# Causal zeros set on GpSimd after the exponential in eleven of sixteen attention steps, instead of by mask matmuls

## What is computed

```
x = layernorm(x + attention(x))        # 16 heads of 16, causal
x = layernorm(x + experts_by_token(x)) # one of 4 by token id
x = layernorm(x + moe_ffn(x))          # router, best of 4 experts, 1024 wide
```

```
scores = einsum('bhqd,bhkd->bhqk', Q, K) / sqrt(16)
scores = where(causal, -inf, scores)        # causal: key index > query index
attn = softmax(scores, axis=-1)
out = einsum('bhqk,bhkd->bhqd', attn, V)
```

## Time and profile before

| | us |
|---|---|
| runs, median (lowest to highest) | 321.23 (320.64 to 323.58), 3 runs |
| profiled execution, its own time | 322.61 |
| its span, first to last instruction | 320.8 |
| TensorE busy | 248.8 (78%) |
| VectorE busy | 185.1 (58%) |
| ScalarE busy | 130.3 (41%) |
| GpSimd busy | 73.9 (23%) |
| mean granted TensorE clock | 0.909 |

### The profile page before, as it was taken

How to read it: one execution, slowest core, us unless ns; L and a number is a source line. 1 busy time by engine, 2 the same in 40 slices (tenths; PEclk the granted TensorE clock), 3 DMA queues, 4 the chain that set the end, 5 groups by cost and what they waited for, 6 DMA issues and landing times.

```text
span 320.8 us, 5861 instructions
## 1 busy us (share of the span) xinstructions
PE 248.8 (78%) x1991; PEld 165.2 (52%) x1992; DVE 185.1 (58%) x406; ACT 130.3 (41%) x218; POOL 73.9 (23%) x125
## 2 busy tenths in 40 slices
PE   4795789887986773447797537679999999999990
PEld 3364556555664551124676432236666656666570
DVE  3868577776889447813776758023544445455441
ACT  4451565855946674305575300033323213333210
POOL 8400000100141303810333268100222111222222
PEclk9799699999999998596999556599999999999997
DMA  6999072422253741448200011240000000000000
GB/s 201 339 326 284 6 261 68 127 73 67 68 164 84 215 133 39 191 144 298 102 3 0 2 42 68 89 115 2 16 18 1 2 11 16 16 16 16 9 13 2
DMA packets 18055, 29.29 MB, mean 91 GB/s; under 512 B 2796, under 2 KB 13550, under 8 KB 18032
## 3 DMA queue, kind: packets, MB, share of 16 engines
q1 hardware_dynamic: 16592, 25.81, 26.4%
q0 software_dynamic: 1440, 3.17, 2.7%
HBM read 19.69 MB, written 10.03 MB: 93 GB/s over the span
## 4 chain that ended last, share of the span: by engine, by line
PE 54%; DVE 16%; issue 9%; ACT 7%; DMA 5%; POOL 5%; SPq 3%; POOLq 0%; ACTq 0%; DVEq 0%
PE ps L1103 34%; DVE arena L848 3%; PE ps L1408 3%; ACT wf_hi L480 3%; PE ps L1213 2%; PE ps L1174 2%; PE ps L1109 2%; POOL sorted L422 2%; POOL sorted L451 2%; SPq L335 2%; DMA ring<-wqkvT 1%; PE ps L1170 1%; DVE wf_lo L686 1%; DVE arena L845 1%; DMA arena<-Wf 1%
## 5 line engine op out<-in xcount | busy, mean ns | idle before, releaser
L1103 PE MATMUL ps<-wf_hi,arena 128*128 x336 | 82.0, 329 | 2.8 <-DVE arena L1031 1.6
L1103 PE MATMUL ps<-wf_lo,arena 128*128 x168 | 55.2, 328 | 0.0
L1103 PEld LDWEIGHTS ps<-wf_hi,arena 128*128 128x128 f16 x336 | 32.8, 98 | 26.8 <-issue 6.7
L639 ACT ACTIVATE arena<-ps 128x512 f32<-128x512 f32 x22 | 13.2, 598 | 65.3 <-PE ps L1103 65.3
L1031 DVE SCALAR_TENSOR_TENSOR arena<-ps,arena 128x512 f32<-128x512 f32 x22 | 15.2, 692 | 25.3 <-ACT arena L639 13.5
L1109 PE MATMUL ps<-wf_hi,ones 128*128 128x512 f16 x51 | 18.9, 545 | 12.4 <-issue 6.1
L686 DVE SCALAR_TENSOR_TENSOR wf_lo<-ring,wf_hi 128x1024 f16<-128x1024 f32 x17 | 20.5, 1219 | 8.6 <-ACT wf_hi L480 8.6
L1103 PE MATMUL ps<-xT_hi,arena 128*128 x88 | 20.3, 295 | 5.4 <-DVE arena L991 4.6
L1103 PEld LDWEIGHTS ps<-wf_lo,arena 128*128 128x128 f16 x168 | 16.4, 98 | 9.4
L1103 PE MATMUL ps<-arena,xT_hi 128*128 128x512 f16 (+1 forms) x64 | 17.2, 358 | 4.9 <-DVE arena L805 2.3
L457 POOL TENSOR_SCALAR veps<-mv 128x1 f32<-128x1 f32 x11 | 2.5, 226 | 79.6 <-DVE mv L1051 79.6
(11 more groups left out here) (202 smaller groups left out, 525.6 us busy)
## 6 DMA issues: line engine op xcount, KB each, us to landing
ring<-Wf SPq DMA_DIRECT2D x17, 512.0 KB, 3.8
sorted<-fill SPq DMA_DIRECT2D x1, 4515.0 KB, 22.0
arena<-Wf SPq DMA_DIRECT2D x7, 512.0 KB, 6.0
arena<-sorted SPq DMA_DIRECT2D x22, 129.0 KB, 2.1
sorted<-fill SPq DMA_DIRECT2D x1, 1419.0 KB, 7.2
ring<-xT SPq DMA_DIRECT2D x4, 256.0 KB, 5.5
X<-x_tok SPq DMA_DIRECT2D x1, 1024.0 KB, 8.4
ring<-ctxT SPq DMA_DIRECT2D x2, 512.0 KB, 3.9
```

The source lines that it names most:

```text
L639: a.activation(sg[:, half * 512:(half + 1) * 512], ps[:, 2 * half, :], ACT.Silu, scale=1 / W_SCALE).then_inc(sg3, 1)
L1103: last = t.matmul(dst, xs(k), ws(k), start=(k == 0 and m == 0), stop=(k == nk - 1 and m == 2))
```

## The change

In the first eleven steps (`CUT = STEPS - AHEAD = 11`) `scores_T` has no mask matmul: each head's matmul starts its own accumulation, and the exponential is taken of all entries. GpSimd then sets the entries with key index above query index to zero in `Pf`, by one affine select in place for each of the two diagonal blocks (128 x 512 float32), as soon as the exponential that wrote it is done, and signals `p_cut`. `values(n)` waits for both. In the last five steps the mask matmuls stay. `scores`, for the maxima, keeps its masks everywhere.

On GpSimd the selects take their places in the order of steps. The memset moves behind step 4's selects, `inv_std` of batch 0 stands ahead of step 8's, and the first `scatter2` moves behind step 10's.

```diff
+CUT = STEPS - AHEAD
...
-            pool.wait_ge(st_rdy, 2 * NG)
-            g.memset(QT[0][DK * 2:SLOT, 1::2, :].bitcast(F32), 0.0).then_inc(row_z, 1)
+            def causal(n):
+
+                for part, c in enumerate((0, 2)):
+                    pool.wait_ge(exped, 2 * n + part + 1)
+                    block = Pf[n % 2][:, c].rearrange("p (a t) -> p a t", a=G)
+                    g.affine_select(out=block, in_=block, compare_op=ALU.is_ge, fill=0.0, base=0,
+                                    pattern=[[0, G], [1, P]], channel_multiplier=-1).then_inc(p_cut, 1)
+
+            for n in range(CUT):
+                if n == 2 * NG:
+                    pool.wait_ge(mv1, TB)
+                    inv_std(mv[:, :, 1], TB, rs1)
+                causal(n)
+                if n == NG:
+                    pool.wait_ge(st_rdy, 2 * NG)
+                    pool.wait_ge(p_cut, 2 * n + 2)
+                    g.memset(QT[0][DK * 2:SLOT, 1::2, :].bitcast(F32), 0.0).then_inc(row_z, 1)
+                    pool.wait_ge(row_z, 1)
             pool.wait_ge(filled, 32)
             pool.wait_ge(pos_rdy, 1)
-            for b in range(B - 2):
+            scatter2(0)
+            for b in range(1, B - 2):
                 pool.wait_ge(mv1, TB * (b + 1))
                 inv_std(mv[:, :, 1], TB, rs1)
                 scatter2(b)
...
-                    diag = qt == kt
+                    diag = qt == kt and n >= CUT
                     if diag:
                         t.matmul(ps[:, bank, :], identB[:, :], maskT[:, :, :].rearrange("p a k -> p (a k)"),
                                  start=True, stop=False)
...
                 pe.wait_ge(exped, 2 * n + 2)
+                if n < CUT:
+                    pe.wait_ge(p_cut, 2 * n + 2)
                 if n >= 1:
                     pe.wait_ge(o_sb, n)
```

More of the change, by code:

```diff
@@ L198, in build @@
             "s_rdy", "maxed", "mT_done", "m_row"))
-        st_rdy, exped, av_rdy, o_sb, oS_rdy, o_norm = (sem(n) for n in (
-            "st_rdy", "exped", "av_rdy", "o_sb", "oS_rdy", "o_norm"))
+        st_rdy, exped, p_cut, av_rdy, o_sb, oS_rdy, o_norm = (sem(n) for n in (
+            "st_rdy", "exped", "p_cut", "av_rdy", "o_sb", "oS_rdy", "o_norm"))
         oT_rdy, oT_hi, oT_lo, wo_rdy, res1, bn1, mv1, rs1, x1_rdy = (sem(n) for n in (
```

## The result

| | before | after |
|---|---|---|
| median of four runs, us | 320.97 | 325.39 |
| its runs, us | 320.64 to 323.58 | 323.33 to 327.88 |
| profiled execution, us | 322.61 | 325.79 |
| its span, us | 320.8 | 324.1 |
| its mean granted clock | 0.909 | 0.894 |

The ratio is 1.013, with a 95% interval from 1.0091 to 1.0169. Two more sets of the same changed kernel, each beside the kernel before on its chip, gave 1.0051 (1.0005 to 1.0096, 10 runs) and 1.0075 (1.004 to 1.0111, 12 runs). The forecast was 321.0 us and no change, in a range of 319.0 to 322.8. The sign is certain; by these ratios the size lies between 0.5 and 1.3%, by the medians between 1.0 and 1.4%.

The account below looks back on a forecast made before the run. Attention was taken as bound by a chain through TensorE, ScalarE and VectorE, with TensorE waiting part of the time. Terms -0.43 - 0.44 + 0.6 = -0.27 us on the 321.23 median gave 321.0 us, range 319.0 to 322.8.

Parts of the forecast that it names:

- A mask matmul taken out of such a step makes the wait longer and nothing else shorter: Most attention steps, where TensorE already waits 0.21 us before scores: removing mask matmuls there gains nothing.
- the working of step 0: Step 0 at the low clock: 0.86 us of masks removed, half lost to slower following projection, leaving 0.43 us gained.
- The gains of steps 0 and 6: The only steps with removed mask matmuls on the chain: gains of 0.43 and 0.44 us, 0.87 together.
- The port: Steps 8 and 9: GpSimd selects hold VectorE's L686 at the shared SBUF port, costing 0.6 us.
- The middle of the bounds: L686's loss to the selects: 0 if not held, 0.3 by one, 0.9 by both; 0.6 us taken.
- the slower rival: Steps 8 and 9: VectorE, with L901 held too, loses more than TensorE gains; 321.9 us, chance 0.13.
- The selects' size: Twenty-two GpSimd selects of 0.58 to 0.64 us each, about 13 us in all, on an engine with idle time.
- What was counted at nothing: values' wait for p_cut, selects in steps 0 to 7, the moved scatter and memset: 0 us each.
- The rival that TensorE's time counts in every step: All attention steps: the 5.26 us of removed mask matmuls shortens the kernel to 316.0 us; chance 0.07.

Follow-up runs that it names:

- e2: Against the kernel before: mask matmuls of the first eleven steps out, no selects, zeroing above the diagonal left out; 323.97 us, ratio 1.0061.
- e4: Against the full change: step 9's selects wait for step 8's L704, first scatter goes ahead of step 10's selects; 326.14 us, ratio 1.0113 to before.
- g1: The full change, unedited, run again on a chip shared with three variants; 325.13 us, ratio 1.0075 to the kernel before.
- r2: The full change, unedited, run again for a second profile; 326.24 us, ratio 1.0051 to the kernel before.
- f2: Same kernel as e2, run again on another chip; 321.91 us, ratio 0.9957 to the kernel before.
- g2: Same kernel as e4, run again on the chip of g1; 325.02 us, ratio 1.0069 to the kernel before.
- h2: Same kernel as e4, paired on one chip with h1, from which it differs by 22 mask matmuls taken out; 325.15 us, ratio 1.006 to before.
- r1: The kernel before, unedited, run again for a second profile; 322.21 us, ratio 0.9992.
- e1: Against the kernel before: selects, their waits and GpSimd's new order added, all 32 mask matmuls kept; 323.89 us, ratio 1.0033.
- f1: Against e1: step 9's selects wait for step 8's L704, first scatter ahead of step 10's selects, masks still kept; 322.48 us, ratio 0.9994 to before.
- h1: Same kernel as f1, paired on one chip with h2; 323.73 us, ratio 1.002 to the kernel before.
- f3: Against the full change: e4's order, fillers ahead of step 5's transpositions, step 12 and last projection, values ahead of second output transposition; 324.40 us, ratio 1.0042 to before.
- f4: Against the kernel before: values placed as in f3, fillers ahead of step 12 and the last output projection; 323.10 us, ratio 1.0008.
- g3: Against the full change: four filler matmuls ahead of step 5's output transpositions, on the chip of g1; 324.97 us, ratio 1.0069 to before.

## Why the prediction was wrong

**The step that failed** is the sentence "A mask matmul taken out of such a step makes the wait longer and nothing else shorter", which priced the longer wait at nothing. The first half is right: TensorE's waits before `scores` grew from 0.21 to 0.64 us. But waiting longer had a price, since TensorE was granted its lower level more often, and with the selects there too that cost more time than the matmuls had. Eight profiled kernels with masks out and no filler in step 5 show 4.66 us for step 5 four times (after, e2, e4, g1) and 3.01 four times (r2, f2, g2, h2); five with masks kept (the profiles of before, r1, e1, f1, h1) and five with fillers show 3.01 always. (f3 and f4, where `values` stands elsewhere, are left out.) Summed from 33 to 125 us, the low stretches come to 3.8 us in r1 and 6.8 in before, e1, f1 and h1, which keep their masks; to 13.7 in after, r2, e4 and g1, 10.6 in e2, 8.7 in f2, 7.4 in g2 and 6.4 in h2, which don't; and to 7.8 to 13.7 in the five with fillers. One profile can't place its kernel: h2 has less than most with masks, and from 125 us on, where these versions have the same instructions, the same profiles have anything from 43 to 55 us. The rival on the clock wasn't among those named, though the earlier trace rows had the level of 0.54 in them and the working of step 0 used it. The forecast asked what becomes of work at the low clock, and never whether the change would bring more of it.

**The gains of steps 0 and 6** were 0.52 and 0.42 us, forecast 0.43 and 0.44: right, for a pair of profiles that both have step 0 at the low clock.

**The port** was mis-sized: +0.6 forecast, 0.95 measured as the growth of that stretch in all six profiles that have the selects in the changed order. The middle of the bounds was taken, and L901 was left out of it. The argument was that its rate per element doesn't show a second port. The rate doesn't exclude it: the two L919 took 604 and 720 ns beside the selects and 408 to 414 ns elsewhere. The Trainium skill (SBUF — State Buffer, "Who interferes with whom") lists `tensor_scalar` among the operations that can take both ports. The trace agrees with it, and the row was read for more than it says. This was the mechanism of the slower rival; its held time of 0.95 us is just over the 0.87 at which it was to decide, so it cancels the gains, which were 0.94. It doesn't make the kernel slower by itself.

**The selects' size** was right: 0.58 to 0.64 us forecast, 22 of them between 627 and 926 ns with a median of 637, and 2.50 us for four in a row. GpSimd's busy time grew by 15.2 us, forecast about 13.

**What was counted at nothing** held for `values`, which waited for L432 in none of the profiles, for L686 of steps 0 to 7, none of which was held, and for the scatter and the memset.

So the sum by its own steps is -0.52 - 0.42 + 0.95, about 0, and the chain without the clock gives no change. The first profile adds 1.65 + 0.46 + 1.10 = 3.21 us of work at the low clock and 0.39 of the transfer. That the masks taken out lower the clock is shown by the granted clocks of seven sets of runs on five chips. That this costs time is shown by the middle column above and by h1 and h2, and so only with the selects there. The rival that TensorE's time counts in every step fell with it: attention ended later, not 5 us earlier.

**What stays open.** Which execution gets a low stretch where isn't told by the wait before it: 1.93 us stands ahead of both outcomes in step 5, and of the kernels with masks kept, r1 and f1 have a low stretch between 73 and 80 us, the others not. Why either repair alone wins next to nothing in the median though each shows in the profile, and both together about 1 to 2 us, wasn't found. Nor was the effect of the masks out alone (1.0061 and 0.9957 on two chips), nor what the selects do to TensorE once the masks are gone. The last projection, whose own masks no version touches, goes by the moment of a fall that comes between 122 and 128 us in all seventeen profiles without fillers there. It took 2.74 us in the twelve where the fall came first, and 1.65 to 2.21 us in the five where the fall came 0.6 to 1.2 us behind its start (before, r1, f1, h1 and g3). The fall came first in all eight with masks out and no filler, in three of the four with step 5 filled, and in one of the five with masks kept (e1). What sets its moment isn't shown.

No version beat the kernel before: f1 equals it within 0.3%, and f2, 0.4% faster in one set, leaves out the zeroing and didn't repeat.

## What to carry to other kernels

Matmuls that lie beside the chain weren't free to remove here: before pricing such a removal at nothing, look in the windows at the granted clock around the waits that would grow, and name "the clock falls more often" as a rival with its price, the chain's work there at half speed. Don't add up halves that were measured apart: here neither half alone, in the mended order, had a cost that could be measured, and both had 2.4 us. Keep a new GpSimd instruction like this select away from VectorE's L919 and L704 of the chain, which read SBUF alone: holding step 9's selects back gave back 0.75 of 0.95 us. Behind L704 they stood beside L887, which reads PSUM and SBUF and took 0.42 us there in e4, as it does without a select. Judge a change of about 1% by many runs on more than one chip: two profiles of one kernel, e4 and h2, have spans of 325.0 and 320.1 us.

## What the runs showed that was not expected

- VectorE's L919 with one SBUF tensor and two scalars per partition is held by a GpSimd select: 604 and 720 ns for 408 to 414, and one L704 of 1644 ns for 1220. The two L919 lost 0.52 us together and the two-tensor L704 0.42, although L919 runs no faster per element.
- With the selects in both, a kernel with 22 matmuls less ran at a mean granted clock of 0.907, and the same with them at 0.917 (medians of the runs of h2 and h1), and was 1.4 us slower.
- The place of a low stretch isn't fixed for a kernel: after has it at 67 to 72 and 95 to 99 us, r2 at 92 to 96 and 102 to 110. Step 5 takes either 3.01 or 4.66 us.
- Four filler matmuls (1.02 us) in a wait of 1.93 us kept the clock at its full level there in all five profiles that had them and the old place of `values`; four of the eight without them kept it too.
